# MLP block of a two-layer kernel: three float32r products in place of each float32 product, with the splits on ScalarE and GpSimd

## What is computed

```python
attn_out = out.reshape(B, N, N, E) @ Wo
h = x_in + attn_out
h = _layer_norm(h, ln_agg_g, ln_agg_b)
mlp = jax.nn.relu(h @ W1 + b1) @ W2 + b2
h = mlp + h
return _layer_norm(h, ln_out_g, ln_out_b)
```

## Time and profile before

| | |
|---|---|
| time, median of 3 runs | 2487.22 us (2486.73 to 2491.69) |
| profiled execution | 2488.98 us, span 2487.2 us |
| busy in the span | PE 2141.8 us (86%), DVE 2003.4 (81%), ACT 1298.0 (52%), POOL 1012.7 (41%) |
| mean granted TensorE clock | 0.970 |
| MLP block | 1135 to 1487 us |

### The profile page before, as it was taken

How to read it: one execution, slowest core, us unless ns; L and a number is a source line. 1 busy time by engine, 2 the same in 40 slices (tenths; PEclk the granted TensorE clock), 3 DMA queues, 4 the chain that set the end, 5 groups by cost and what they waited for, 6 DMA issues and landing times. The chain is left out here.

```text
span 2487.2 us, 42555 instructions
## 1 busy us (share of the span) xinstructions
PE 2141.8 (86%) x16632; PEld 1396.7 (56%) x16632; DVE 2003.4 (81%) x2384; ACT 1298.0 (52%) x2834; POOL 1012.7 (41%) x513
## 2 busy tenths in 40 slices
PE   8999867776787676665999978999999999999998
PEld 7877412231232221113777756777777777777776
DVE  4426699979988999993877757888888888888886
ACT  3337467757756774541233334555555555555553
POOL 1103689979988999990110001111112111111111
PEclk9999889999999999997999998999999999999999
DMA  6668332124121212102233205232222223333332
GB/s 233 233 215 242 97 61 36 28 52 85 20 51 28 36 20 45 20 12 86 96 98 88 88 32 105 69 73 71 74 75 72 75 77 92 92 93 91 86 78 60
DMA packets 302504, 204.44 MB, mean 82 GB/s; under 512 B 202721, under 2 KB 280033, under 8 KB 297697
## 3 DMA queue, kind: packets, MB, share of 16 engines
q1 hardware_dynamic: 293600, 168.17, 27.4%
q0 software_dynamic: 8704, 33.56, 3.7%
HBM read 133.76 MB, written 67.90 MB: 81 GB/s over the span
## 5 line engine op out<-in xcount | busy, mean ns | idle before, releaser
L330 DVE TENSOR_TENSOR att_av<-att_att,att_v2ps 128x2816 f32<-128x2816 f32 (+2 forms) x288 | 775.5, 2749 | 59.5 <-PE att_bank L509 56.9
L330 POOL TENSOR_TENSOR att_av<-att_att,att_v2sb 128x1280 f32<-128x1280 f32 x256 | 744.6, 2936 | 73.7 <-PE att_bank L509 69.6
L509 PE MATMUL att_bank<-att_av,att_w 128*32 128x512 f32 x4096 | 546.9, 618 | 233.4 <-DVE att_av L330 190.2
L509 PEld LDWEIGHTS att_bank<-att_av,att_w 128*32 128x32 f32 x4096 | 136.7, 111 | 581.0 <-issue 283.4
L650 ACT ACTIVATE att_ev<-att_bank 128x512 f32<-128x512 f32 x512 | 297.3, 595 | 284.7 <-PE att_bank L509 215.3
L1693 DVE SCALAR_TENSOR_TENSOR mb_cv<-mb_bank,mb_cw,mb_cv 128x504 f32<-128x504 f32 (+2 forms) x480 | 342.7, 729 | 126.4 <-ACT mb_cv L1516 121.4
L1336 POOL TENSOR_TENSOR mb_rstd<-mb_ms,mb_neghalf 128x4 f32<-128x4 f32 x32 | 32.3, 1008 | 793.8 <-DVE mb_ms L1737 793.8
L1397 PE MATMUL mb_bank<-mb_xT_hi,dt_win_hi 128*128 128x512 f32 x576 | 242.1, 420 | 36.8 <-DVE mb_cv L1693 35.4
L1455 PE MATMUL mb_bank<-mb_wf,mb_y 128*128 128x256 f32 x1024 | 245.2, 387 | 0.8 <-DVE mb_y L1733 0.8
L1397 PE MATMUL mb_bank<-mb_xT_lo,dt_win_hi 128*128 128x512 f32 x576 | 229.2, 398 | 0.0
L1397 PE MATMUL mb_bank<-mb_xT_hi,dt_win_lo 128*128 128x512 f32 x576 | 228.8, 397 | 0.0
(11 more groups left out here) (182 smaller groups left out, 3331.6 us busy)
## 6 DMA issues: line engine op xcount, KB each, us to landing
att_xin<-in_x SPq DMA_DIRECT2D x32, 512.0 KB, 4.4
qk_t<-att_qk POOLq DMA_DIRECT2D x16, 1024.0 KB, 5.1
v<-att_vs POOLq DMA_DIRECT2D x16, 1024.0 KB, 5.2
mixed_t<-att_ev SPq DMA_DIRECT2D x1024, 8.0 KB
mb_dAb<-dA_rows SPq DMA_DIRECT2D x32, 512.0 KB, 5.6
mb_dAb<-dA_cols SPq DMA_DIRECT2D x32, 512.0 KB, 6.2
att_q<-qk_t SPq DMA_DIRECT2D x8, 1024.0 KB, 9.9
att_kb<-qk_t SPq DMA_DIRECT2D x128, 64.0 KB, 2.0
```

The costliest lines, as they stand in the source:

```text
L330: return eng.tensor_tensor(av[t % 2][:, :, d0:d1, :], a.unsqueeze(2).broadcast_to((P, 2, d1 - d0, N)), v2.unsqueeze(1).broadcast_to((P, 2, ...
L509: mm = pe.matmul(bank[r % NB][s * M:(s + 1) * M, :], w[i // WB % 2][:, i % WB, s, :], av[r // 2 % 2][:, i % 2, s * STRIP_D:(s + 1) * STRIP ...
```

## The change

- `wo`, `w1`, `w2`, `att`, `hid` and `hT` get float32r parts hi and lo, and each of the products with Wo, W1 and W2 becomes three float32r products.
- The hi parts: of the weights by a copy on GpSimd, of `att` by a copy on ScalarE (`att_hi`), of `hid` by a second relu on ScalarE ahead of the full one, of `hT` by the existing copy on ScalarE.
- The lo parts (value less hi): weights, `att` and `hid` on GpSimd, `hT` on VectorE (`low_of_hT`, from the bank).
- b2 and the second norm's bias (`be2`) are added by GpSimd (`add_b2`, `add_be2`) instead of VectorE; `o_ready` now comes from GpSimd, and VectorE's gain signals `o_gained`.
- The products with W2 are reordered (`times_w2`), and TensorE waits for hi and lo of each tile by itself.
- SyncE stores chunk c - 1 where it stored c, loads of `att` also wait for `att_lo`, and the second load of `win` moves from c = 5 to c = 8. The split of `win` is spread over c = 4 to 6 and 10 to 12.

```diff
--- before.py
+++ after.py
-        hT = [sb(f"hT{u}", [P, KT, CHUNK]) for u in range(2)]
+        hT = {n: [sb(f"hT{u}_{n}", [P, KT, CHUNK], F32R) for u in range(2)] for n in ("hi", "lo")}
+        wo_, w1_, w2_ = [{n: sb(f"{w}_{n}", shape, F32R) for n in ("hi", "lo")}
+                         for w, shape in (("wo", [P, KT, E]), ("w1", [P, KT, F]), ("w2", [P, FT, E]))]
+        att_ = {n: sb(f"att_{n}", [P, KT, CHUNK], F32R) for n in ("hi", "lo")}
         hid = sb("hid", [P, FT, CHUNK])
+        hid_ = {n: sb(f"hid_{n}", [P, FT, CHUNK], F32R) for n in ("hi", "lo")}
...
                 need(sp, added, 2 * c - 2)
+                need(sp, att_lo_ready, c - 1)
...
                 load(c + 2, c % 2)
-                store(c, c % 2)
+                if c > 0:
+                    store(c - 1, (c - 1) % 2)
                 if c == 2:
                     load_win(0)
-                if c == 5:
+                if c == 8:
                     load_win(1)
+            store(NCHUNK - 1, (NCHUNK - 1) % 2)
...
+            def split_weights(n, w, parts):
+                pool.tensor_copy(parts["hi"][:, :, :], w[:, :, :]).then_inc(w_split, 1)
+                pool.wait_ge(w_split, 2 * n + 1)
+                pool.tensor_tensor(parts["lo"][:, :, :], w[:, :, :], parts["hi"][:, :, :], ALU.subtract).then_inc(w_split, 1)
+
+            def att_lo(c):
+                if c < NCHUNK:
+                    pool.wait_ge(att_hi_ready, c + 1)
+                    need(pool, wo_done, 2 * c)
+                    pool.tensor_tensor(att_["lo"][:, :, :], att[c % 2][:, :, :], att_["hi"][:, :, :], ALU.subtract)\
+                        .then_inc(att_lo_ready, 1)
+
+            def hid_lo(c):
+                need(pool, w2_done, 2 * c)
+                for i, m in enumerate(ORDER):
+                    pool.wait_ge(hid_ready, FT * c + i + 1)
+                    pool.tensor_tensor(hid_["lo"][:, m, :], hid[:, m, :], hid_["hi"][:, m, :], ALU.subtract)\
+                        .then_inc(hid_lo_ready, 1)
+
+            def add_be2(c):
+                pool.wait_ge(o_gained, c + 1)
+                pool.tensor_tensor(o[c % 2][:, :, :], o[c % 2][:, :, :], wide(row["be2"]), ALU.add).then_inc(o_ready, 1)
+
+            def add_b2(c):
+                if c < NCHUNK:
+                    pool.wait_ge(h_ready, c + 1)
+                    need(pool, o_gained, c - 1)
+                    pool.tensor_tensor(hb[c % 2][:, :, :], h[c % 2][:, :, :], wide(row["b2"]), ALU.add).then_inc(b2_added, 1)
+
+            def win_hi(d):
                 pool.wait_ge(win_loaded, 16 * d + 16)
                 for k in range(KT):
                     pool.tensor_copy(carried.win_hi[d][:, k], win[:, k]).then_inc(win_split, 1)
+
+            def win_lo(d, k):
                 pool.wait_ge(win_split, 2 * KT * d + KT)
-                for k in range(KT):
-                    pool.tensor_tensor(carried.win_lo[d][:, k], win[:, k], carried.win_hi[d][:, k], ALU.subtract)\
-                        .then_inc(win_split, 1)
-                pool.wait_ge(win_split, 2 * KT * d + 2 * KT)
+                pool.tensor_tensor(carried.win_lo[d][:, k], win[:, k], carried.win_hi[d][:, k], ALU.subtract)\
+                    .then_inc(win_split, 1)
+
+            pool.wait_ge(wo_loaded, 16)
+            split_weights(0, wo, wo_)
+            att_lo(0)
+            pool.wait_ge(w_loaded, 32)
+            split_weights(1, w1, w1_)
+            att_lo(1)
+            split_weights(2, w2, w2_)
+            pool.wait_ge(rows_loaded, 16 * 6)
+            add_b2(0)
+            for c in range(NCHUNK):
+                att_lo(c + 2)
+                hid_lo(c)
+                if c > 0:
+                    add_be2(c - 1)
+                add_b2(c + 1)
+                for d in range(2):
+                    if c == 4 + 6 * d:
+                        win_hi(d)
+                    if c in (5 + 6 * d, 6 + 6 * d):
+                        win_lo(d, c - 5 - 6 * d)
+            add_be2(NCHUNK - 1)
...
             def times_wo(c, u):
-                pe.wait_ge(in_loaded[u], (c // 2) * 32 + 32)
-                need(pe, hT_ready, 2 * c)
+                pe.wait_ge(att_lo_ready, c + 1)
+                need(pe, hT_lo_ready, 2 * c)
                 for t in range(TT):
-                    for k in range(KT):
-                        mm = pe.matmul(WO_[t // 2][:, (t % 2) * E:(t % 2 + 1) * E], att[u][:, k, t * P:(t + 1) * P],
-                                       wo[:, k, :], start=(k == 0), stop=(k == KT - 1))
+                    for n, (k, xn, wn) in enumerate([(k, xn, wn) for k in range(KT) for xn, wn in SPLIT]):
+                        mm = pe.matmul(WO_[t // 2][:, (t % 2) * E:(t % 2 + 1) * E], att_[xn][:, k, t * P:(t + 1) * P],
+                                       wo_[wn][:, k, :], start=(n == 0), stop=(n == 3 * KT - 1))
...
-                        mm = pe.matmul(HID_[m][:, :], w1[:, k, m * P:(m + 1) * P], hT[u][:, k, :],
-                                       start=(k == 0), stop=(k == KT - 1))
+                    for n, (k, xn, wn) in enumerate([(k, xn, wn) for k in range(KT) for xn, wn in SPLIT]):
+                        mm = pe.matmul(HID_[m][:, :], w1_[wn][:, k, m * P:(m + 1) * P], hT[xn][u][:, k, :],
+                                       start=(n == 0), stop=(n == 3 * KT - 1))
...
-                for t in range(TT):
-                    for i, k in enumerate(ORDER):
-                        if t == 0:
-                            pe.wait_ge(hid_ready, FT * c + i + 1)
-                        mm = pe.matmul(OUT_[t // 2][:, (t % 2) * E:(t % 2 + 1) * E], hid[:, k, t * P:(t + 1) * P],
-                                       w2[:, k, :], start=(i == 0), stop=(i == FT - 1))
-                    if t % 2:
-                        mm.then_inc(w2_done, 1)
-                    if t == 2:
-                        turn_h(c + 1, 1 - u)
+                times_w2(c, 0, "hi")
+                times_w2(c, 2, "hi")
+                times_w2(c, 0, "lo")
+                times_w2(c, 1, "hi")
+                times_w2(c, 1, "lo").then_inc(w2_done, 1)
+                times_w2(c, 2, "lo")
+                turn_h(c + 1, 1 - u)
+                times_w2(c, 3, "hi")
+                times_w2(c, 3, "lo").then_inc(w2_done, 1)
+
+            def times_w2(c, t, part):
+
+                for i, k in enumerate(ORDER):
+                    if t == 0:
+                        pe.wait_ge(hid_hi_ready if part == "hi" else hid_lo_ready, FT * c + i + 1)
+                    for wn in ("hi", "lo") if part == "hi" else ("hi",):
+                        mm = pe.matmul(OUT_[t // 2][:, (t % 2) * E:(t % 2 + 1) * E], hid_[part][:, k, t * P:(t + 1) * P],
+                                       w2_[wn][:, k, :], start=(part == "hi" and i == 0 and wn == "hi"),
+                                       stop=(part == "lo" and i == FT - 1))
+                return mm
...
-            pe.wait_ge(w_loaded, 32)
+            pe.wait_ge(w_split, 6)
...
+            def att_hi(c):
+                if c < NCHUNK:
+                    act.wait_ge(in_loaded[c % 2], (c // 2) * 32 + 32)
+                    need(act, wo_done, 2 * c)
+                    act.activation(att_["hi"][:, :, :], att[c % 2][:, :, :], ACT.Copy).then_inc(att_hi_ready, 1)
...
                     act.wait_ge(hid_done, FT * c + i + 1)
+                    act.activation(hid_["hi"][:, m, :], HID_[m][:, :], ACT.Relu, bias=b1[:, m:m + 1]).then_inc(hid_hi_ready, 1)
                     act.activation(hid[:, m, :], HID_[m][:, :], ACT.Relu, bias=b1[:, m:m + 1]).then_inc(hid_ready, 1)
...
+            att_hi(0)
+            att_hi(1)
+            act.wait_ge(rows_loaded, 16 * 6)
             root(0, 0)
             copy_hT(0, 0)
             for c in range(NCHUNK):
+                att_hi(c + 2)
...
-                chain.link(dve.tensor_tensor(out[:, :, :], out[:, :, :], wide(gain), ALU.mult))
+                gained = dve.tensor_tensor(out[:, :, :], out[:, :, :], wide(gain), ALU.mult)
+                if n == 1:
+                    gained.then_inc(o_gained, 1)
+                    return
+                chain.link(gained)
...
+                need(dve, b2_added, c - 1)
...
+            def low_of_hT(c, u):
+                if c < NCHUNK:
+                    for k in range(KT):
+                        dve.wait_ge(hT_hi_ready, 2 * c + k + 1)
+                        dve.tensor_tensor(hT["lo"][u][:, k, :], WO_[k][:, :], hT["hi"][u][:, k, :], ALU.subtract)\
+                            .then_inc(hT_lo_ready, 1)
...
-                dve.tensor_tensor(hb[u][:, :, :], h[u][:, :, :], wide(row["b2"]), ALU.add).then_inc(b2_added, 1)
...
+                    if half == 0:
+                        low_of_hT(c + 1, 1 - u)
...
             front(0, 0)
+            low_of_hT(0, 0)
```

(20 more changed lines are left out.)

3 lines of the change are left out of this document (1 added, 2 removed).

## The result

| | before | after |
|---|---|---|
| time, median | 2488.03 us (2486.73 to 2491.69, 4 runs) | 2552.65 us (2547.78 to 2554.87, 4 runs) |
| ratio | | 1.0255, 95% interval 1.0235 to 1.0274 |
| profiled execution | 2488.98 us, span 2487.2 | 2547.78 us, span 2546.0 |
| mean granted TensorE clock | 0.970 | 0.961 |

The change makes the kernel slower by 64.6 us by the medians and by 58.8 us by the two profiled executions. The forecast was 2533 us and slower, in a range of 2474 to 2556.

A forecast was written before the change was run, and what follows sets the result against it. TensorE's stream bounds the MLP loop now; the change makes a four-engine ring with 22.1 us turns. Turns 31.4, start 6, table loads 3.8 and win loads 4.8 add 46.0 us: 2535.0 profiled, 2533 median, range 2474 to 2556.

The forecast's parts named there:

- a ring of four engines: MLP loop: the change hangs four engines into a ring, whose turn becomes 22.1 us instead of 19.86.
- the load wait: ScalarE's att_hi waits for load(c+3), issued behind a store that waits for GpSimd's be2; alone it gives turns of 20.0 us.
- an att_hi released by TensorE: Sign on ScalarE's timeline that would make the forecast wrong; expected was release by the load, some 2 us after Wo's end.
- TensorE's sum: TensorE's own work per chunk: 17.3 us, 2.5 less than before, with 256-column products every 0.127 us.
- a = 6.0: Start of ScalarE's att_hi, 6.0 us after the end of a chunk's low_of_hT, with load wait and port clash.
- The shared port: GpSimd's operations and VectorE's gain and bias alternate: 0.9 us on the last hid_lo, 1.2 on be2, turn 22.1 us.
- The tensor_scalar: By the skill's rule, VectorE's eight L1049 of a turn could each meet GpSimd: some tenths more, inside the range.
- The turns together: Loop: 14 turns at 2.24 us more, +31.4; three ScalarE table loads +3.8; two big loads of win +4.8.
- The start: First chunk: att_hi and att_lo +3.5, low_of_hT +0.7, port clash with the first norm +1.8 (0 to 4.8): +6 us.
- (a): Rival: the load wait comes but the port costs nothing on the path; turn 20.0 us, 2502 us; chance 0.18.
- (b): Rival: short ring, ScalarE never waits for the load; turn 18.6 us, 2478 us, at best 2456; chance 0.25.
- (c): Rival: TensorE is worse, 256-column products at 0.22 us or clock falling in gaps; turn about 23.3, 2550 us; chance 0.12.

The follow-up runs named there:

- the memsets: Changed kernel with GpSimd's att_lo, hid_lo, be2 and b2 in the loop replaced by equally long memsets of a scratch tile: 2513.63 us, ratio 1.0099.
- be2 first: Changed kernel with GpSimd doing be2(c-1), then att_lo(c+2), ahead of hid_lo(c), with the same work: 2521.75 us, ratio 1.0136.
- w1 split behind the norm: Kernel before with only W1 as three products and b2, be2 on GpSimd, w1's split held until the first norm's bias is done: 2479.98 us.
- the best order: Changed kernel with GpSimd doing be2(c-1), hid_lo(c), then, after VectorE's bias of h, att_lo(c+2) and b2(c+1): 2505.05 us, ratio 1.0066.
- W1 alone: Kernel before with only W1 as three float32r products, w1 split by GpSimd ahead of the loop: 2480.65 us, ratio 0.9964.

## Why the prediction was right, and where it was off

The direction held, and so did half of the mechanism: a ring of four engines takes the place of TensorE's stream, its turn is longer than TensorE's own work, and GpSimd's operations stretch VectorE's. The other half, the load wait, did not set the turn. By the forecast's own sign ("an att_hi released by TensorE") it was wrong there: between 1190 and 1520 us TensorE released three att_hi. That the turn came near (22.1 forecast; of the fifteen, seven had a mean of 22.4, see "The turns together") is in part luck: a wait that wasn't there and a clash that was larger nearly cancel. The size was short, by 12.8 us on the profiled executions (+58.8 against +46.0). By its steps:

- **TensorE's sum.** Right, a little high. Products of 256 columns start every 0.12 us (forecast 0.127) at the full clock (the single-column rate by its own figures, 0.70 through 7, is 0.10 where it wrote 0.11; no term uses it):

```profile
1349.42 0.28 PE L931 MATMUL mlp_bank<-mlp_wo_hi,mlp_att_lo 128*128 128x256 f32 x1
1349.54 0.28 PE L931 MATMUL mlp_bank<-mlp_wo_lo,mlp_att_hi 128*128 128x256 f32 x1
1349.66 0.28 PE L931 MATMUL mlp_bank<-mlp_wo_hi,mlp_att_hi 128*128 128x256 f32 x1
```

  By the formula of the Trainium skill for an isolated product (TensorE: Matmul & The Clock Gate, Back-to-back issue gap) it would be 0.109 us; the trace doesn't bear that out here either. TensorE's own turn of 17.3 was never reached by any kernel; 18.4 was.
- **The load wait.** The term of the sum that failed. The forecast had att_hi at a = 6.0, some 2 us after Wo's end, released by the load. It came at 1328.85 - 1325.50 = 3.35 us behind the end of low_of_hT:

```profile
1328.85 1.06 ACT L1034 ACTIVATE mlp_att_hi<-mlp_att 128x1024 fp32r<-128x1024 f32 x1 [0.42 <-DMA mlp_xin<-in_x]
```

  The load released it, but just as Wo was done: the three that TensorE released had an idle time of 0.34 to 0.43 us before them. Of the eight that the load released, six had 0.42 to 0.77, and the two behind the loads of `win` 2.34 and 3.11. The load is late by its own reckoning, as the memsets show (4.91 against 4.8), but the turn had grown by more than the load was late, and so it was absorbed.
- **The shared port.** The failing step is the order "They alternate: hid_lo, gain, hid_lo, bias, be2". The order on the chip was hid_lo, gain, be2, bias. GpSimd's be2, issued at 1341.96 during the gain of h, ran as soon as the gain was done, ahead of the bias, and what the forecast put on be2 and, by it, on the load fell on the bias and on turning h. Three clashes were left out: att_lo on the gain of o (in five chunks), the normalisation of h, and softplus, whose VectorE instructions lie in chunks 3, 6, 10, 12 and 14 (five, not the seven of the kernel's description) and took 10.8 us in the fifteen turns instead of 2.2. In the turn shown the gain of o and L1187 make the first norm, the root on ScalarE and the last two relus late: the moments came at 1337.87, 12.4 us behind low_of_hT where the forecast had 9.3. In place of 0.9 + 1.2 us, VectorE lost 4.6 us a turn, and 0.6 more in softplus.
- **The tensor_scalar.** The normalisation of h took 1.43 us a chunk more (1.1 without the first), and the memsets did not free it. The Trainium skill (SBUF — State Buffer, Who interferes with whom) says both: tensor_scalar in a two-port mode and GpSimd exclude each other, while VectorE's tensor_tensor with two SBUF inputs is held only by a GpSimd instruction that reads SBUF. With this the traces agree: beside memsets gains and bias took 1225 ns and the normalisation 746 against 409. That these tensor_scalar run in a two-port mode is shown by no run. The forecast had put this rule at some tenths.
- **The turns together.** Forecast 31.4, with table loads 3.8 and the loads of `win` 4.8: 40.0 us. Measured 49.9. By turn: the one behind the second load of `win` took 27.9 us, the first 20.0, and the six in which GpSimd also splits `win` 23.9 on average; the other seven (2 to 5, 9, 11 and 15) had a mean of 22.4. Against these seven the load cost 5.5 us and the six turns 9 us, where the forecast had the splits of `win` in GpSimd's slack and 3.8 for table loads. What the splits themselves cost isn't shown: with be2 first these six were no longer than the others.
- **The start.** Forecast +6, measured +9.6. The clash was put at 1.8 us, within 0 to 4.8. It was 5.6 us: GpSimd's w1 split, att_lo(1) and w2 split follow each other without a gap and held the four normalisations of the first chunk:

```profile
1155.17 7.01 DVE L1131 TENSOR_SCALAR mlp_h<-mlp_h,mlp_mv,mlp_rstd 128x256 f32<-128x256 f32 x4
```

  The run with w1 split behind the norm confirms this cause for the smaller case.
- **The end.** Forecast 0; 58.8 - 59.5 = -0.7, as good as nothing.
- **The rivals.** (a) and (b) were not what happened, but their turns are what comes once the clash on gains and bias is taken away: 19.8 against 20.0 us a turn with the load wait, 18.4 against 18.6 without it. (c) had the nearest time, 2550, for reasons that aren't borne out: the products don't cost 0.22 at the full clock, and what ends the turn is the bias, not a product at the lower clock. The clock did fall, in the gaps of the ring: the granted clock was 1.00 (2.4 GHz) from 1336.2 to 1341.0 and 0.50 (1.2 GHz) from 1341.2 to 1344.4, after TensorE had stood for 1.92 and for 0.65 us. Products start every 0.12 us and then every 0.21:

```profile
1338.83 0.39 PE L1008 MATMUL mlp_bank<-mlp_w_hi,mlp_hid_hi 128*128 128x256 f32 x1 [1.92 <-ACT mlp_hid_hi L1073]
...
1340.80 0.28 PE L1008 MATMUL mlp_bank<-mlp_w_hi,mlp_hid_hi 128*128 128x256 f32 x1
1340.91 0.28 PE L1008 MATMUL mlp_bank<-mlp_w_lo,mlp_hid_hi 128*128 128x256 f32 x1
...
1341.21 0.41 PE L1008 MATMUL mlp_bank<-mlp_w_lo,mlp_hid_hi 128*128 128x256 f32 x1
1341.42 0.41 PE L1008 MATMUL mlp_bank<-mlp_w_hi,mlp_hid_lo 128*128 128x256 f32 x1
```

  In this turn TensorE then still waited 1.06 us for the bias, so the slower products cost nothing. That the lower clock costs something in other turns is not excluded: from 1190 to 1440 us the granted clock was 0.93 in the changed kernel, 0.95 with be2 first, 0.97 with the memsets and 0.99 in the best order, and no run takes the clock and the shorter turn apart.

Two things stay open. A kernel in which the normalisation of h no longer meets GpSimd (on ScalarE, say) was not tried; it is the largest clash left in the best order. And what the split of `win`, softplus and the table loads each cost in the long turns was not separated.

## What to carry to other kernels

Work that is moved to GpSimd is not free just because GpSimd is idle: lay it out against VectorE's timeline, and place it where VectorE reads PSUM or takes statistics. Here the order of GpSimd's work alone decided 48 us of 65. Where two engines exclude each other, reckon both orders of the clash and ask which of the two ends the turn; and when a wait and a stretch lie on parallel arms, don't add them, the longer one absorbs the other. Before turning all products of a ring into a cheaper form, try the one whose split can be paid outside it: W1 alone gave a gain that all three together turned into a loss.

## What the runs showed of the hardware

- A tensor_scalar of 128x256 float32 with its two scalars per partition was held beside GpSimd's subtractions, casts and memsets alike: four took 1.38 us alone, up to 5.05 in the loop with be2 first, and 7.01 beside the weight splits. The forecast had expected tenths.
- Short VectorE instructions got through one at a time between GpSimd's. The four normalisations of 7.01 us start at 1155.17, 1156.29, 1158.64 and 1159.68, and each ends 0.15 us behind one of four GpSimd instructions in a row; the last ends at 1162.18, w2's subtraction (1159.69 to 1162.03) before it.
- float32r products of 256 columns start every 0.12 us at the full clock, 0.21 at half: 24 of them for Wo and 48 for W2 are worth about 0.6 and 1.1 us a chunk against the float32 products (3.46 and 6.9 us).
- Memsets of 1390 and 2560 float32 per partition took 1.30 and 2.24 us on GpSimd, about what a subtraction of 512 and of 1024 takes (1.26 and 2.38): a stand-in of equal length without the reads.
